# Linear-attention denominator as one 128x128 block matmul with a DMA round trip, and wider states, in a two-branch attention kernel on one core

## The reference

```python
xn = _layernorm(x)
# linear branch, per head of 32, phi(t) = elu(t) + 1
S_kv = S_kv + einsum('bhd,bhe->bhde', k_t, v_t)     # running state, 32 x 32 per head
z    = z + k_t
num  = einsum('bhd,bhde->bhe', q_t, S_kv)
den  = einsum('bhd,bhd->bh', q_t, z)[..., None] + 1e-6
out  = (num / den) @ wo
# softmax branch
q = (q / norm(q) + query_embedding) * softplus(temperature)
h = softmax(q @ k.T / sqrt(32)) @ v
out = h * gates(h) @ Wp.T + bp
```

## Time and profile before

| | |
|---|---|
| median of three runs | 3962.01 us |
| the profiled execution, its time | 3962.01 us |
| its span | 3960.1 us |
| PE, PEld busy | 3731.3, 1702.9 us |
| DVE, ACT, POOL busy | 3349.4, 2668.0, 436.5 us |
| mean granted clock | 0.988 of full |

### The profile page before, as it was taken

How to read it: one execution, slowest core, us unless ns; L and a number is a source line. 1 busy time by engine, 2 the same in 40 slices (tenths; PEclk the granted TensorE clock), 3 DMA queues, 4 the chain that set the end, 5 groups by cost and what they waited for, 6 DMA issues and landing times.

```text
span 3960.1 us, 147413 instructions
## 1 busy us (share of the span) xinstructions
PE 3731.3 (94%) x65855; PEld 1702.9 (43%) x65856; DVE 3349.4 (85%) x3595; ACT 2668.0 (67%) x2617; POOL 436.5 (11%) x229
## 2 busy tenths in 40 slices
PE   2789999999999999999999999999999999999999
PEld 1544443444344444444444444444444444444333
DVE  5668988888888988888898888889788788888887
ACT  3457777777777667667677667667666766766663
POOL 3101010010001001101101100111000110100121
PEclk8889999999999999999999999999999999999999
DMA  5322212221132223223222323323222222222223
GB/s 206 113 76 60 73 53 61 61 71 56 57 85 86 74 86 91 75 69 95 81 75 79 93 63 93 91 64 92 67 65 77 75 83 61 84 63 61 80 84 109
DMA packets 364209, 315.81 MB, mean 80 GB/s; under 512 B 158168, under 2 KB 312248, under 8 KB 362932
## 3 DMA queue, kind: packets, MB, share of 16 engines
q1 hardware_dynamic: 362852, 297.93, 25.3%
q10 hardware_dynamic: 720, 8.39, 0.5%
HBM read 230.74 MB, written 75.48 MB: 77 GB/s over the span
## 4 chain that ended last, share of the span: by engine, by line
PE 72%; DVE 10%; issue 9%; ACT 7%; DMA 1%; SPq 1%; DVEq 0%; POOL 0%; ACTq 0%; POOLq 0%
PE ps L1067 29%; PE ps L1231 17%; PE ps L1217 15%; ACT prob L899 5%; DVE acc L1768 5%; PE ps L1132 3%; PE ps L1161 2%; PE ps L1101 2%; PE ps L1155 1%; DVE zc L1714 1%; ACT r L845 1%; DVE y L1789 1%; SPq L431 1%; DVE qb L1671 1%; DVE phqT L1708 1%
## 5 line engine op out<-in xcount | busy, mean ns | idle before, releaser
L899 ACT ACTIVATE prob<-ps 128x2048 f32<-128x2048 f32 x1024 | 1923.8, 1879 | 600.5 <-PE ps L1217 596.6
L1768 DVE TENSOR_TENSOR acc<-acc,prob 128x2048 f32<-128x2048 f32 x896 | 2056.5, 2295 | 102.7 <-ACT prob L899 87.6
L1231 PE MATMUL ps<-prob,v 128*32 128x512 f32 x8192 | 1092.0, 605 | 0.0
L1217 PE MATMUL ps<-q_hi,k_hi 32*128 32x512 f16 x4096 | 420.1, 384 | 95.8 <-ACT prob L899 90.1
L1067 PE MATMUL ps<-x_hi,w_hi 128*32 128x512 f16 x4096 | 413.2, 384 | 1.9 <-ACT dl L855 1.2
L1067 PE MATMUL ps<-x_lo,w_hi 128*32 128x512 f16 x4096 | 412.2, 382 | 0.0
L1067 PE MATMUL ps<-x_hi,w_lo 128*32 128x512 f16 x4096 | 411.9, 382 | 0.0
L1217 PE MATMUL ps<-q_hi,k_lo 32*128 32x512 f16 x4096 | 410.1, 374 | 0.6 <-issue 0.6
L1217 PE MATMUL ps<-q_lo,k_hi 32*128 32x512 f16 x4096 | 409.7, 374 | 0.0
L1231 PEld LDWEIGHTS ps<-prob,v 128*32 128x32 f32 x8192 | 161.3, 107 | 434.1 <-issue 434.0
L1067 PE MATMUL ps<-wop_hi,fin 128*32 128x512 f16 x4096 | 343.0, 381 | 4.7 <-DMA y<-in_x 3.0
(11 more groups left out here) (263 smaller groups left out, 4288.2 us busy)
## 6 DMA issues: line engine op xcount, KB each, us to landing
x_hi<-xhi_scratch SPq DMA_DIRECT2D x64, 512.0 KB, 6.2
x_lo<-xlo_scratch SPq DMA_DIRECT2D x64, 512.0 KB, 7.4
x_in<-in_x SPq DMA_DIRECT2D x64, 256.0 KB, 7.0
rq<-rq_scratch SPq DMA_DIRECT2D x64, 256.0 KB
rdl<-rdl_scratch SPq DMA_DIRECT2D x64, 256.0 KB
y<-in_x SPq DMA_DIRECT2D x64, 256.0 KB, 6.0
out<-y SPq DMA_DIRECT2D x64, 256.0 KB, 5.9
rden<-rden_scratch SPq DMA_DIRECT2D x63, 256.0 KB
```

The source lines that it names most:

```text
L899: s_.activation(prob[i % 3][:], ps[:, 0:HG, :], ACT.Exp, bias=-SHIFT, scale=inv_c[:, g:g + 1] if wide else 1.0 / CQK).then_inc(exped, 2)
L1217: last = t_.matmul(bank[h], kk[rows32(h), cols128(kt)], qq[rows32(h), :], start=(kk is kh and qq is qh), stop=(kk is kl and not wide))
L1231: last = t_.matmul(bank[OUT][rows32(h), :], v[m // NB % 2][:, kt, rows32(h)], prob[i % 3][:, h, :], start=(kt == 0), stop=(kt == TT - 1))
L1768: v_.tensor_tensor(acc[:], acc[:], prob[i % 3][:], ALU.add).then_inc(summed, 1)
```

## The change

The four matmuls of four column tiles each in `linear_den` are replaced by one matmul of the whole array: the stationary operand is `blockden`, 128x128, four blocks of 32x32 that hold the constant of `heads_v`, and the moving operand is zc, 512 columns. So X1 holds each head's denominator on all of its 32 partitions. `keep_dl` copies all 128x512 of it into `rdl`. `turn_dl` and `keep_rdl` are gone. In their place SP runs `pack` on `rdl` at slot 0: one row of each head to DRAM scratch, and back as 16x128 into `rdl_c`, which DVE inverts in slot 2 (`invert_dl`). `spread` is as before, into the same `rdl`.

The states `st` are kept as 128x128 with the heads' 32x32 blocks on the diagonal and zeros elsewhere. `key_values` multiplies each tile's 128 columns of v, `keep_kv` copies the four diagonal blocks into a `kvm` that is cleared once, `states` adds 128x128, and the state part of `numerators` contracts over all 128 partitions.

Left out of the diff below: the names of the semaphores.

```diff
@@ -239,7 +239,7 @@
-        heads_v, ones_v = sb("heads_v", [P, HG]), sb("ones_v", [P, HD])
+        blockden, ones_v = sb("blockden", [P, P]), sb("ones_v", [P, HD])
         crow_ones = sb("crow_ones", [P, BN], F16)
@@ -306,9 +306,9 @@
         am = sb("am", [P, HG, BT, P])
-        st = sb("st", [P, NST, HD])
-        kvm = sb("kvm", [P, BT, HD])
-        dl, rdl_c, rdl, o1 = sb("dl", [P, HG, BT]), sb("rdl_c", [HG * BT, P]), sb("rdl", [P, BN]), sb("o1", [P, BN])
+        st = sb("st", [P, NST, P])
+        kvm = sb("kvm", [P, BT, HG, HD])
+        rdl_c, rdl, o1 = sb("rdl_c", [HG * BT, P]), sb("rdl", [P, BN]), sb("o1", [P, BN])
         o_hi, o_lo = sb("o_hi", [P, BN], F16), sb("o_lo", [P, BN], F16)
@@ -569,6 +568,9 @@
                     if kt == 0:
+                        if p is not None:
+                            sp.wait_ge(dl_kept, p + 1)
+                            pack(rdl_c, rdl_d, rdl, dl_out, dl_in, p)
                         if f is not None and s < LIGHT:
@@ -582,7 +584,7 @@
                         if p is not None:
-                            sp.wait_ge(rdl_kept, p + 1)
+                            sp.wait_ge(rdl_done, p + 1)
                             spread(rdl, rdl_d, rdl_c[:], rdl_out, rdl_in, p, o1_ready)
@@ -851,16 +853,19 @@
                 act.wait_ge(dl_mm, p + 1)
-                act.wait_ge(rdl_turned, p)
-                s_.activation(dl[:].rearrange("p h t -> p t h"), X1[:, 0:BT * HG].rearrange("p (t h) -> p t h", t=BT), ACT.Identity,
-                              bias=eps1[:, 0:1]).then_inc(dl_kept, 1)
+                act.wait_ge(o1_ready, p)
+                s_.activation(rdl[:], X1, ACT.Identity, bias=eps1[:, 0:1]).then_inc(dl_kept, 1)
 ...
                     act.wait_ge(state_ready, states_after(n - 1))
-                s_.activation(kvm[:].rearrange("p t e -> p (t e)"), X1[:, 0:BT * HD], ACT.Copy).then_inc(kv_kept, 1)
+                act.wait_ge(kvm_cleared, 1)
+                for h in range(HG):
+                    ins = s_.activation(kvm[rows32(h), :, h, :], X1[rows32(h), :].rearrange("p (t n) -> p t n", t=BT)[:, :, rows32(h)],
+                                        ACT.Copy)
+                ins.then_inc(kv_kept, 1)
@@ -1103,13 +1108,7 @@
                 pe.wait_ge(pz_ready, n + 1)
-                for j in range(BT):
-                    last = by_columns(X1[:, j * HG:(j + 1) * HG], zc[:, cols128(j)], heads_v[:], True, True)
-                last.then_inc(dl_mm, 1)
-
-            def turn_dl(p):
-                pe.wait_ge(rdl_done, p + 1)
-                t_.transpose(X0[0:HG * BT, 0:P], dl[:].rearrange("p h t -> p (h t)"), ident[:]).then_inc(rdl_turned, 1)
+                t_.matmul(X1, blockden[:], zc[:], start=True, stop=True).then_inc(dl_mm, 1)
@@ -1137,9 +1136,7 @@
                 for j in range(BT):
-                    for h in range(HG):
-                        last = t_.matmul(X1[rows32(h), j * HD:(j + 1) * HD], pk[:, j, rows32(h)], vl[:, j, rows32(h)],
-                                         start=True, stop=True)
+                    last = by_columns(X1[:, cols128(j)], pk[:, j, :], vl[:, j, :], True, True)
                 last.then_inc(kv_done, 1)
@@ -1158,8 +1155,8 @@
                     for h in range(HG):
-                        last = t_.matmul(X1[rows32(h), cols128(j)], st[rows32(h), i % NST, :], phqT[rows32(h), cols128(j)], start=False,
-                                         stop=True, skip_group_check=True)
+                        last = t_.matmul(X1[rows32(h), cols128(j)], st[:, i % NST, rows32(h)], phqT[:, cols128(j)], start=False, stop=True,
+                                         skip_group_check=True)
                 last.then_inc(num_done, 1)
@@ -1250,13 +1247,10 @@
                             pe.wait_ge(am_ready, 2 * p + 2)
-                            turn_dl(p)
                         if mp is not None:
 ...
                             total(mp)
-                    if kt == 2 and p is not None:
-                        pe.wait_ge(rdl_kept, p + 1)
                     if kt == 2 and n is not None:
@@ -1655,7 +1649,8 @@
             v_.tensor_scalar(ones_v[:], ones[:, 0:HD], den_one[:, 0:1], None, ALU.mult)
-            v_.tensor_scalar(heads_v[:], headmask[:], v1_one[:, 0:1], None, ALU.mult)
+            v_.tensor_scalar(blockden[:].rearrange("p (h e) -> p h e", h=HG), headmask[:].unsqueeze(2).broadcast_to([P, HG, HD]),
+                             v1_one[:, 0:1], None, ALU.mult)
             link(v_.tensor_scalar(wg_hi[:], wg_raw[:], s_g[:, 0:1], None, ALU.mult))
@@ -1736,16 +1731,11 @@
                     dve.wait_ge(state_ready, i + 1)
-                    v_.tensor_tensor(st[:, (i + 1) % NST, :], st[:, i % NST, :], kvm[:, j, :], ALU.add).then_inc(state_ready, 1)
+                    v_.tensor_tensor(st[:, (i + 1) % NST, :], st[:, i % NST, :], kvm[:, j].rearrange("p h e -> p (h e)"), ALU.add).then_inc(state_ready, 1)
             def invert_dl(p):
-                dve.wait_ge(dl_kept, p + 1)
-                v_.reciprocal(dl[:], dl[:]).then_inc(rdl_done, 1)
-
-            def keep_rdl(p):
-                dve.wait_ge(rdl_turned, p + 1)
-                dve.wait_ge(rdl_out, p * 16)
-                v_.tensor_copy(rdl_c[:], X0[0:HG * BT, 0:P]).then_inc(rdl_kept, 1)
+                dve.wait_ge(dl_in, (p + 1) * 16)
+                v_.reciprocal(rdl_c[:], rdl_c[:]).then_inc(rdl_done, 1)
@@ -1849,15 +1839,13 @@
                         add_up(mp, TT - 1)
-                    if kt == 0 and p is not None:
-                        invert_dl(p)
                     if kt == 1 and p is not None:
 ...
                         if p is not None:
-                            keep_rdl(p)
+                            invert_dl(p)
                         if s <= LIGHT and gate_block(s - 1) is not None:
@@ -1932,6 +1920,7 @@
+            v_.memset(kvm[:], 0.0).then_inc(kvm_cleared, 1)
             wide_reg = dve.alloc_register("wide_dve")
```

More of the change, by code:

```diff
@@ L356, in build @@
         o_stored, h_stored = sem("o_stored"), sem("h_stored")
-        den_out, den_in, rden_out, rden_in, rdl_out, rdl_in, rq_out, rq_in = (
-            sem(n) for n in ("den_out", "den_in", "rden_out", "rden_in", "rdl_out", "rdl_in", "rq_out", "rq_in"))
+        den_out, den_in, rden_out, rden_in, dl_out, dl_in, rdl_out, rdl_in, rq_out, rq_in = (
+            sem(n) for n in ("den_out", "den_in", "rden_out", "rden_in", "dl_out", "dl_in", "rdl_out", "rdl_in", "rq_out", "rq_in"))
         settled, pool_const, dve_link, act_const, pool_pow = (
@@ L365, in build @@
             sem(n) for n in ("wsq_ready", "n2_done", "n2_kept", "ak_ready", "whi_split", "wlo_split"))
-        e_turned, setup_done, headmask_ready = (sem(n) for n in ("e_turned", "setup_done", "headmask_ready"))
+        e_turned, setup_done, kvm_cleared, headmask_ready = (sem(n) for n in ("e_turned", "setup_done", "kvm_cleared", "headmask_ready"))
         ln_stat, ln_pow, ln_done, x_summed = sem("ln_stat"), sem("ln_pow"), sem("ln_done"), sem("x_summed")
@@ L381, in build @@
             sem(n) for n in ("ql_proj", "kl_proj", "ql_part", "kl_part", "phq_done", "phk_done", "phk_turned", "pk_kept"))
-        scan_done, pz_ready, dl_mm, dl_kept, rdl_done, rdl_turned, rdl_kept = (
-            sem(n) for n in ("scan_done", "pz_ready", "dl_mm", "dl_kept", "rdl_done", "rdl_turned", "rdl_kept"))
+        scan_done, pz_ready, dl_mm, dl_kept, rdl_done = (sem(n) for n in ("scan_done", "pz_ready", "dl_mm", "dl_kept", "rdl_done"))
         at_done, am_ready, kv_done, kv_kept, state_ready, num_done, num_kept, o1_ready, ohi_done, olo_done = (
```

## The result

After: 4006.22 us, median of four runs (4003.08 to 4007.56). Before, in the same comparison: 3962.22 us. The ratio is 1.0109, 95% interval 1.0092 to 1.0127: slower by 44 us, where the forecast said 64. The profiled execution took 4005.88 us, with a span of 4004.0.

What follows compares the result with a forecast made beforehand. The prediction took PE's small work, in slots where PE finishes after the exponential, as the bound. Its terms, 42.6 + 22.5 - 7.3 + 6.6 = +64.4 us on 3962.0, gave 4026 us, range 3990 to 4057.

Steps and rivals of the forecast that it cites:

- Denominator matmul: Slot 15 on PE: the wide matmul takes 1.07 us instead of 0.36, +0.71 us in 60 steps, +42.6 us.
- The cheap rival: Slot 15: the wide matmul adds only 0.2 us instead of 0.71, giving 3995 us; chance 0.08.
- key_values: Slot 13 on PE: 128 columns instead of 32, +0.58 us in 16 early steps, +0.30 in 44 late, +22.5 us.
- State numerators: Slot 3 on PE: the tile-shape switch between the two parts goes, -0.12 us in 61 steps, -7.3 us.
- Prologue: Steps -4 to -1, without exponentials: slower wide matmul and longer ACT copy, 4 x 1.65 = +6.6 us.
- turn_dl: Slot 1: 0.21 us of PE work leaves, but the exponential ends the slot, so 0.
- The end that was named: Slot 1: the most PE could win between the exponential's end and the score, 60 x 0.12 = -7 us.
- ACT, DVE and the queues: Longer ACT copies, DVE's reciprocal and wider adds, SP's transfers: all taken as covered, costed at nothing.
- The stall rival: Slot 2: transfers take twice 1.9 us and DVE stands waiting, 0.5 us x 60 = +30, 4056 us; chance 0.10.
- The faster rival: Slots 13 and 15: additions lie hidden under the exponential and cost nothing, 3948 us; chance 0.05.
- the one of no change: Slots 13 and 15: about half of the room needed to hide the additions exists, 3962 within 8 us; chance 0.05.
- Late steps 0.9 us longer and early ones 1.2: Predicted trace sign: late steps lengthen by 0.9 us, the 16 early ones by 1.2 us.

## Why the prediction was right, and where its sum was too high

The direction, the place and the mechanism hold: PE's small work is paid where PE ends the slot, and slots 15, 13 and 14 paid 59 us of it. The sum was 64.4 and the traces' spans differ by 43.9. Term by term:

- **Denominator matmul, +42.6 predicted, +39.4 measured.** The distance to the next score is 1.05 us (forecast 1.07); 0.66 us a step over all slots 15, in place of 0.71. The single steps read 0.69; in every fourth step it is less. The cheap rival is refuted by the doubled matmul, at 0.87 us for two passes of 512 columns. By the Trainium skill, "TensorE: Matmul & The Clock Gate", section "Back-to-back issue gap" (about 131 ns a matmul of 512 columns, given without a type of operand), an estimate for the two instructions is 0.26 us: for these f32 operands the measured 0.87 us is more than three times that, and the measurement decides.
- **key_values, +22.5 predicted, +19.6 measured.** 0.99 us to `key_query`, exactly as forecast, and +0.58 in early steps. The late steps' price, 0.30, was read off one step with a wait for y of 0.21 us, where a mean wait (12.0 us in 44) is 0.27. The wide form fills that much more: 0.23 was measured.
- **State numerators, -7.3 predicted, -8.1 measured.** 0.87 and 0.99 us, for 0.88 and 1.00. The Trainium skill, "TensorEngine Tiling (Array Packing)", section "Key Properties", says that a change of tile mode needs a drain; the trace agrees, with 0.13 us for the one that is gone.
- **Prologue, +6.6 predicted, +6.3 measured.** That the sizes agree is in part luck. From the start of the denominator's matmul to ACT's copy it took 0.68 us in each of the four prologue steps before, and 1.17, 2.11, 2.12 and 2.12 us after; with the copy's 0.40 us that is 6.4 us in the four, as the prediction had it. But the same product as four column tiles has a prologue only 0.4 us longer than before, and the kernel with the matmul doubled 3.8 us. So something else in the prologue moves by several us from kernel to kernel; DVE's waits for the trip, 7.5 us there in the change, are a candidate that no run isolates. And 2.0 us of it were given back at once. The profile's windows around the first score, before (first fence) and after (second); the columns are the window, its length, busy time of each engine, the granted clock and the DMA share with GB/s:

```profile
240.00:244.00 4.00, 4.00 (x62) 1.50 (x60) 2.59 (x8) 2.17 (x2) 0.55 (x1) 0.50 0.00 0
244.00:248.00 4.00, 4.00 (x51) 1.08 (x41) 0.00 (x0) 1.76 (x2) 0.00 (x0) 0.88 0.01 4
```

```profile
240.00:244.00 4.00, 2.67 (x25) 2.38 (x24) 1.88 (x2) 0.00 (x0) 0.00 (x0) 0.50 0.00 0
244.00:248.00 4.00, 4.00 (x28) 1.36 (x30) 2.95 (x7) 0.88 (x2) 0.15 (x1) 0.60 0.00 0
248.00:252.00 4.00, 4.00 (x64) 1.33 (x56) 1.20 (x3) 3.13 (x3) 0.40 (x1) 1.00 0.02 4
```

  Step 0 starts at a granted clock of 0.50, 1.2 GHz, in both kernels. Before, most of slot 0 ran at it (projections 0.43 us apart, up to 244.64); after, only the first score did, and the projections were 0.22 apart from the start. By the means of the windows the clock rose near 245.0, 4.7 us after the first score's start, before, and near 247.2, 0.6 us after it, in the change. The prediction had stopped at the first score and not followed the clock beyond it.
- **turn_dl, 0 predicted, -4.0 measured (slot 1 as a whole -5.9).** This is the step that failed in kind. The prediction said that "the exponential ends it" because score 1 started 0.12 us after the exponential's end. But the earlier trace rows show `total` with its full 1.00 us before that score and no wait in brackets: PE ended slot 1, by 0.07 us. The other 1.9 us lie in three steps (s = 12, 15 and 60) and are not its work: with the wide states alone, `turn_dl` in place, the same steps are 1.5 us shorter too. Their cause stays open. The end that was named was -7.
- **ACT, DVE and the queues, 0 predicted.** The kernel without the round trip shows it for the softmax steps; in the prologue it stays open. The stall rival is out at one trip, and its own arithmetic, a lead of 1.0 us with 2.3 us of idle time behind it, stands near the 0.6 and 2.6 us that the second trip measured.
- **Not in the sum: -4.1 us of pauses in slots 4 to 6**, and -1.3 us of rest and tail. The pauses end behind late packets of the instruction queue in every kernel, and differ by -6.7 to +8.5 us from before to the others; none of it is work that the change adds.

Added up: -3.2 - 2.9 - 0.8 - 0.3 - 2.0 - 5.9 - 4.1 - 1.3 = -20.5 us. About two thirds of it (13.2, with 4.0 of slot 1's 5.9) are places that the prediction had priced, or priced at nothing, each too dear. The pauses stood outside the sum, and their sign here is chance: with those of the doubled matmul the span would have been 12.6 us longer. The faster rival and the one of no change are refuted by slot 15 alone. "Late steps 0.9 us longer and early ones 1.2" came out as 0.69 and 1.04 us (0.66 + 0.23 - 0.13 - 0.07, and 0.66 + 0.58 - 0.13 - 0.07).

## What to carry to other kernels

Read the end of a slot from the wait in brackets, not from how close two starts lie: a producer that ended 0.1 us before may have ended nothing. On an engine that is the bound, count the columns that an instruction moves, not the rows that it contracts or what it saves elsewhere: widening the contraction from 32 to 128 rows was free, widening the moved operand from 4 or 32 to 128 columns a tile was the whole loss. Compare slot by slot, not only totals: PE's pauses moved the totals of these kernels by -7 to +9 us with no edit aimed at them. A change in two halves deserves a run of each: here a part of one was worth 8 us, hidden under 59 us of the rest.

## What the runs showed of the hardware

- A whole-array matmul of f32 operands over 512 columns (two instructions) adds 0.87 us when repeated. `weigh`, eight f32 instructions of 512 columns in four column tiles, takes 0.88 us when its own tile shape follows. The four tiles side by side don't slow each other down: the columns that each moves set the time.
- Leaving a tile shape costs 0.11 to 0.13 us on PE (0.99 against 0.88 us for the same 32 instructions).
- PE's pauses without a releaser (0.2 to 1.8 us) all end 1.2 to 1.7 us after a 16 KB packet of the "instruction" queue landed, 122 of 122 in twelve traces.
- PE's granted clock was 1.2 GHz for about 350 us of the steps with four trips, whose waits on PE are up to 8.2 us long, and for 8 us behind the prologue of the change, whose longest wait for an exponential is 1.1 us.
- A small store and load through DRAM took 3.5 us in series, with SP's issues at 0.53 and 0.33 us. As SP issued them, in the late step shown above:

```profile
1680.34 0.53 SPq L551 DMA_DIRECT2D rdl_scratch<-rdl  x1
1682.04 0.33 SPq L553 DMA_DIRECT2D rdl_c<-rdl_scratch  x1
```

- ACT's copy of a quarter of the partitions takes as long as one of all, 0.27 us, against the `keep_kv` row:

```profile
L866 ACT ACTIVATE kvm<-ps 32x128 f32<-32x128 f32 x256 | 68.8, 269 | 2.3
```
